# Wide cross-attention: output products in three products of high and low parts, raw expert weights loaded one stage later

## What is computed

```python
xn = _layernorm(x, ln_gamma, ln_beta)
q = (xn @ w_q).reshape(B, SQ, 16, 64)
k, v = jnp.split(context @ w_kv, 2, axis=-1)      # 16 heads of 64
attn = softmax(einsum('bqhd,bkhd->bhqk', q * 64 ** -0.5, k))
out = einsum('bhqk,bkhd->bqhd', attn, v).reshape(B, SQ, 1024)
out = (out @ w_out + b_out) * jnp.tanh(gate[0])   # 1024 -> 128
x = x + out
# sparse experts: 8 experts, top 2, hidden 352
gate = silu(einsum('td,ehd->teh', xt, W1)); up = einsum('td,ehd->teh', xt, W2)
```

## Time and profile before

| | |
|---|---|
| median of three runs | 3040.72 us |
| the profiled execution | 3037.89 us, span 3036.1 us |
| mean granted clock of PE | 0.962 |
| busy over the whole span | PE 90%, DVE 69%, POOL 64%, ACT 63% |
| stage x0, both parts | from about 462 to 1262 us |
| first batch and last batch in LAST | 529.2 and 1237.5 us |
| stage f0 begins | 1267.3 us |

### The profile page before, as it was taken

How to read it: one execution, slowest core, us unless ns; L and a number is a source line. 1 busy time by engine, 2 the same in 40 slices (tenths; PEclk the granted TensorE clock), 3 DMA queues, 4 the chain that set the end, 5 groups by cost and what they waited for, 6 DMA issues and landing times. The chain is left out here.

```text
span 3036.1 us, 83028 instructions
## 1 busy us (share of the span) xinstructions
PE 2738.4 (90%) x27974; PEld 2320.1 (76%) x27975; DVE 2097.9 (69%) x4496; ACT 1920.1 (63%) x4300; POOL 1943.3 (64%) x3244
## 2 busy tenths in 40 slices
PE   6999997999999999499997999995899999999996
PEld 5788776888888888388885888883677777777775
DVE  3677655667676766445555999997777878778543
ACT  3566553666666666355553777774878777787762
POOL 4456543456666666416667999984676777867652
PEclk9999997999999999699998999995899999999998
DMA  5566561000000000222222000000000000000000
GB/s 153 169 181 190 170 181 36 2 8 12 14 13 13 12 14 13 71 67 82 81 82 62 1 0 0 0 1 1 1 2 9 5 8 5 5 9 5 8 5 11
DMA packets 204792, 129.08 MB, mean 43 GB/s; under 512 B 13840, under 2 KB 197112, under 8 KB 203896
## 3 DMA queue, kind: packets, MB, share of 16 engines
q1 hardware_dynamic: 196344, 108.80, 12.0%
q0 software_dynamic: 8192, 16.79, 1.9%
HBM read 35.05 MB, written 90.51 MB: 41 GB/s over the span
## 5 line engine op out<-in xcount | busy, mean ns | idle before, releaser
L1552 PE MATMUL a_ps_s<-a_qk,w_ident 128*128 128x256 f32 x1024 | 238.5, 387 | 20.2 <-POOL a_qk L1659 19.1
L1007 POOL TENSOR_TENSOR x_p<-x_p,x_rz 128x1232 f32<-128x1232 f32 x64 | 143.9, 2248 | 165.6 <-DVE x_rz L1116 165.6
L584 DVE TENSOR_REDUCE a_nmax<-a_ps_s 128x4 f32<-128x512 f32 x256 | 164.9, 686 | 113.8 <-PE a_ps_s L373 113.7
L1659 POOL TENSOR_TENSOR a_qk<-a_qkv 128x2048 f32<-128x2048 f32 x64 | 235.6, 3681 | 2.6 <-POOL a_eight L218 1.0
L457 ACT ACTIVATE a_e<-a_ps_s 128x512 f32<-128x512 f32 x256 | 138.9, 595 | 152.8 <-PE a_ps_s L378 152.8
L1552 PEld LDWEIGHTS a_ps_s<-a_qk,w_ident 128*128 128x128 f32 x1024 | 192.0, 193 | 50.4 <-POOL a_qk L1659 22.7
L2374 POOL TENSOR_TENSOR x_sq<-x_e 128x1232 f32<-128x1232 f32 x64 | 143.2, 2238 | 126.2 <-DVE x_t_sq L2533 126.1
L1633 ACT ACTIVATE a_r<-a_o,w_a_rows 128x128 f32<-128x128 f32 x512 | 220.5, 521 | 1.6 <-DVE a_o L1718 1.6
L1387 POOL DMA_INDIRECT f_yg<-f_rows_out,f_index x120 | 114.9, 958 | 152.1 <-DVE f_yo L1467 134.4
L889 ACT ACTIVATE x_uu_hi<-x_ps_u 128x308 fp32r<-128x308 f32 x256 | 101.7, 423 | 106.0 <-PE x_ps_u L752 105.8
L1123 DVE TENSOR_REDUCE x_top<-x_ps_s 128x16 f32<-128x1232 f32 x64 | 91.2, 1424 | 111.2 <-PE x_ps_s L752 111.2
(11 more groups left out here) (626 smaller groups left out, 9742.0 us busy)
## 6 DMA issues: line engine op xcount, KB each, us to landing
f_rows_in<-a_zeros SPq DMA_DIRECT2D x31, 1088.0 KB, 5.4
f_rows_out<-a_zeros SPq DMA_DIRECT2D x31, 1088.0 KB, 8.8
f_xin<-f_rows_in SPq DMA_DIRECT2D x135, 64.0 KB
f_rows_out<-f_yo SPq DMA_DIRECT2D x135, 64.0 KB, 1.6
out<-x SPq DMA_DIRECT2D x16, 256.0 KB, 2.4
f_raw<-in_late_f SPq DMA_DIRECT2D x2, 1408.0 KB, 5.9
w_ctx<-in_ctx SPq DMA_DIRECT2D x1, 2464.0 KB
f_rows_in<-f_xr,f_where POOLq DMA_INDIRECT x128, 2.3
```

The costliest lines, as they stand in the source:

```text
L584: nc.vector.tensor_reduce(nmax[:, u % 2, g, :], ps_s[g][:, :].rearrange("p (t k) -> p t k", t=GROUP), AX.X, ALU.max, negate=True).then_inc ...
L1007: nc.gpsimd.tensor_tensor(wide, wide, rz[:, :].unsqueeze(2).broadcast_to([P, HEADS, K]), ALU.mult).then_inc(p_ready, 1)
L1552: ins = nc.tensor.matmul(ps_s[u % 2][:, 0:HEADS * HEADS], c.ident[:, :], qk[:, u % 2, k, :, :], start=k == 0, stop=k == HD - 1)
L1659: nc.gpsimd.tensor_tensor(qk[:, u % 2, :, :, :], qkv[:, u % UNROLL, 0, :, :].unsqueeze(3).broadcast_to(full), qkv[:, u % UNROLL, 1, :, :]. ...
```

## The change

The operands of LAST are split. The output weights `x0_o` become a pair of F32R tiles. In `wide_weights` DVE scales the raw output weights in place, ACT copies them to the high part, DVE subtracts to the low part. In each slot ACT still copies `ps_o` to the high part of `oT`, now with the semaphore `o_hi_ready`, and DVE makes the low part from `ps_o` minus the high part in two halves, with `oT_ready`. The half 0 stands behind the subtraction of the maximum in DVE's list, the half 1 behind the low parts of `projected` 2 and 3. LAST on PE makes three F32R matmuls for each of the eight float32 ones.

The load of the raw first expert weights leaves stage x0, and stage f0 issues it between the plan and the second weights, into a buffer of its own. ACT waits for it before its first split. The raw copies of keys and context on POOL have one buffer where they had two, with two waits on POOL's own earlier steps.

```diff
@@ wide_weights, scalar
+            act.wait_ge(gated_out, 1)
+            nc.scalar.activation(c.x0_o[0][:, :, :], c.w["x0_out"][:, :, :], ACT.Copy).then_inc(out_hi, 1)
@@ wide_weights, vector
-            nc.vector.tensor_scalar(c.x0_o[:, :, :], c.w["x0_out"][:, :, :], tg[:, 0:1], None, ALU.mult).then_inc(done, 1)
+            nc.vector.tensor_scalar(c.w["x0_out"][:, :, :], c.w["x0_out"][:, :, :], tg[:, 0:1], None, ALU.mult).then_inc(gated_out, 1)
...
+            dve.wait_ge(out_hi, 1)
+            nc.vector.tensor_tensor(c.x0_o[1][:, :, :], c.w["x0_out"][:, :, :], c.x0_o[0][:, :, :].bitcast(F32), ALU.subtract).then_inc(done, 1)
@@ cross_attention_wide
-        oT = sb("oT", [P, 2, PAIRS, P])
+        oT = [sb(f"oT_{n}", [P, 2, PAIRS, P], F32R) for n in ("hi", "lo")]
...
-        @block.sync
-        def _(sp):
-            sp.dma_start(c.f0_raw[:, :], c.inp["late_f0_1"]).then_inc(raw_in, 16)
-            sp.wait_ge(raw_in, 16)
@@ PE, LAST
                     for n in range(PAIRS):
-                        ins = nc.tensor.matmul(ps_y, oT[:, u % 2, n, :], c.x0_o[:, n, :], start=n == 0, stop=n == PAIRS - 1)
+                        hi, lo = (t[:, u % 2, n, :] for t in oT)
+                        nc.tensor.matmul(ps_y, hi, c.x0_o[0][:, n, :], start=n == 0, stop=False)
+                        nc.tensor.matmul(ps_y, hi, c.x0_o[1][:, n, :], start=False, stop=False)
+                        ins = nc.tensor.matmul(ps_y, lo, c.x0_o[0][:, n, :], start=False, stop=n == PAIRS - 1)
                     ins.then_inc(y_ps, 1)
@@ ACT, outputs
-                nc.scalar.activation(oT[:, u % 2, 4 * half:4 * half + 4, :], ps_o[:, :].rearrange("p (n q) -> p n q", n=4),
-                                     ACT.Copy).then_inc(oT_ready, 1)
+                nc.scalar.activation(oT[0][:, u % 2, 4 * half:4 * half + 4, :], ps_o[:, :].rearrange("p (n q) -> p n q", n=4),
+                                     ACT.Copy).then_inc(o_hi_ready, 1)
@@ POOL
+                        wait(pool, keys_lo_ready, s)
...
+                    wait(pool, cx_lo_ready, s)
@@ DVE
+            def outputs(at, half):
+                s, u = at
+                dve.wait_ge(o_hi_ready, 2 * s + half + 1)
+                hi, lo = (t[:, u % 2, 4 * half:4 * half + 4, :] for t in oT)
+                nc.vector.tensor_tensor(lo, ps_o[:, :].rearrange("p (n q) -> p n q", n=4), hi.bitcast(F32), ALU.subtract).then_inc(oT_ready, 1)
...
                                             ALU.subtract).then_inc(d_ready, 1)
+                if at := sl.step(VALUE):
+                    outputs(at, 0)
                 if at := sl.step(ROUTE):
...
                     projected(at, (2, 3))
+                if at := sl.step(VALUE):
+                    outputs(at, 1)
                 if at := sl.step(NORM):
@@ sparse_experts
-        raw = (c.f0_raw, sb("raw2", [D, E * H]))
+        raw = [sb(f"raw{n + 1}", [D, E * H]) for n in range(2)]
...
             sp.dma_start(plan[:, :], c.inp["late_f0_plan"]).then_inc(plan_in, 16)
-            sp.dma_start(raw[1][:, :], c.inp["late_f0_2"]).then_inc(raw_in, 16)
+            for n in range(2):
+                sp.dma_start(raw[n][:, :], c.inp[f"late_f0_{n + 1}"]).then_inc(raw_in[n], 16)
...
             for n in range(2):
-                if n == 1:
-                    act.wait_ge(raw_in, 16)
+                act.wait_ge(raw_in[n], 16)
                 nc.scalar.activation(w_hi[n][:, :], raw[n][:, :], ACT.Copy).then_inc(split_hi, 1)
```

More of the change, by code:

```diff
@@ L637, in wide_weights @@
         tg = sb("tg", [P, 1])
-        ready, gated, a_hi, a_lo, v_hi, done = (sem(n) for n in ("ready", "gated", "a_hi", "a_lo", "v_hi", "done"))
+        ready, gated, a_hi, a_lo, v_hi, done, gated_out, out_hi = (sem(n) for n in ("ready", "gated", "a_hi", "a_lo", "v_hi", "done", "gated_out", "out_hi"))
         block = ctx.enter_context(nc.Block())
@@ L697, in cross_attention_wide @@
         half, minus, one = (c.powers[:, k, 0:4] for k in (0, 1, 3))
-        raw, cx_raw = sb("raw", [P, 2, BATCHES, K]), sb("cx_raw", [P, 2, K])
+        raw, cx_raw = sb("raw", [P, BATCHES, K]), sb("cx_raw", [P, K])
         cx = [sb(f"cx_{n}", [P, 2, K], F32R) for n in ("hi", "lo")]
@@ L724, in cross_attention_wide @@
                  "u_ready", "cx_raw_ready", "cx_hi_ready", "cx_lo_ready", "v_ps", "v_ready", "s_ps", "max_done", "d_ready",
-                 "exp_done", "z_done", "rz_done", "p_ready", "pT_ps", "pT_ready", "o_ps", "oT_ready", "y_ps", "x_done", "biased")
+                 "exp_done", "z_done", "rz_done", "p_ready", "pT_ps", "pT_ready", "o_ps", "o_hi_ready", "oT_ready", "y_ps", "x_done", "biased")
         (xn_ready, xT_ps, xT_ready, x_hi_ready, x_lo_ready, raw_ready, keys_hi_ready, keys_lo_ready, u_ps, u_hi_ready,
          u_ready, cx_raw_ready, cx_hi_ready, cx_lo_ready, v_ps, v_ready, s_ps, max_done, d_ready,
-         exp_done, z_done, rz_done, p_ready, pT_ps, pT_ready, o_ps, oT_ready, y_ps, x_done, biased) = (sem(n) for n in names)
+         exp_done, z_done, rz_done, p_ready, pT_ps, pT_ready, o_ps, o_hi_ready, oT_ready, y_ps, x_done, biased) = (sem(n) for n in names)
         names = ("scaled", "xr_ready", "rT_ps", "rT_ready", "r_ps", "r_ready", "own", "mask_ready", "pos_ps", "pos_ready", "pos_read", "placed",
@@ L993, in slot @@
                         wait(pool, u_ps, 4 * (s - 4))
-                        nc.gpsimd.tensor_copy(raw[:, u // 4, :, :], c.ctx[:, bass.ds(s, BATCHES), :]).then_inc(raw_ready, 4)
+                        wait(pool, keys_lo_ready, s)
+                        nc.gpsimd.tensor_copy(raw[:, :, :], c.ctx[:, bass.ds(s, BATCHES), :]).then_inc(raw_ready, 4)
                         hi, lo = (t[:, u // 4, :, :] for t in keys)
                         pool.wait_ge(raw_ready, s + 4)
-                        nc.gpsimd.tensor_tensor(hi, raw[:, u // 4, :, :], one[:, 0:1].unsqueeze(2).broadcast_to([P, BATCHES, K]), ALU.mult).then_inc(keys_hi_ready, 4)
+                        nc.gpsimd.tensor_tensor(hi, raw[:, :, :], one[:, 0:1].unsqueeze(2).broadcast_to([P, BATCHES, K]), ALU.mult).then_inc(keys_hi_ready, 4)
                         pool.wait_ge(keys_hi_ready, s + 4)
-                        nc.gpsimd.tensor_tensor(lo, raw[:, u // 4, :, :], hi.bitcast(F32), ALU.subtract).then_inc(keys_lo_ready, 4)
+                        nc.gpsimd.tensor_tensor(lo, raw[:, :, :], hi.bitcast(F32), ALU.subtract).then_inc(keys_lo_ready, 4)
                 if sl.fixed and sl.t == SPLIT:
@@ L1005, in slot @@
                     pool.wait_ge(rz_done, s + 1)
+                    wait(pool, cx_lo_ready, s)
                     wide = p[:, u % 2, :, :, :].rearrange("p g j k -> p (g j) k")
                     nc.gpsimd.tensor_tensor(wide, wide, rz[:, :].unsqueeze(2).broadcast_to([P, HEADS, K]), ALU.mult).then_inc(p_ready, 1)
-                    nc.gpsimd.tensor_copy(cx_raw[:, u % 2, :], c.ctx[:, s, :]).then_inc(cx_raw_ready, 1)
+                    nc.gpsimd.tensor_copy(cx_raw[:, :], c.ctx[:, s, :]).then_inc(cx_raw_ready, 1)
                     hi, lo = (t[:, u % 2, :] for t in cx)
                     pool.wait_ge(cx_raw_ready, s + 1)
-                    nc.gpsimd.tensor_tensor(hi, cx_raw[:, u % 2, :], one[:, 0:1].broadcast_to([P, K]), ALU.mult).then_inc(cx_hi_ready, 1)
+                    nc.gpsimd.tensor_tensor(hi, cx_raw[:, :], one[:, 0:1].broadcast_to([P, K]), ALU.mult).then_inc(cx_hi_ready, 1)
                     pool.wait_ge(cx_hi_ready, s + 1)
-                    nc.gpsimd.tensor_tensor(lo, cx_raw[:, u % 2, :], hi.bitcast(F32), ALU.subtract).then_inc(cx_lo_ready, 1)
+                    nc.gpsimd.tensor_tensor(lo, cx_raw[:, :], hi.bitcast(F32), ALU.subtract).then_inc(cx_lo_ready, 1)
                 if at := sl.step(SPLIT):
@@ L1224, in sparse_experts @@
         ps_list = ps_t
-        names = ("raw_in", "w3_in", "plan_in", "split_hi", "split_lo", "late", "own",
+        raw_in = [sem(f"raw_in{n + 1}") for n in range(2)]
+        names = ("w3_in", "plan_in", "split_hi", "split_lo", "late", "own",
                  "value_ready", "list_ps", "listed", "xT_ps", "hi_ready", "lo_ready", "g_ps", "u_ps", "sg_ready", "act_ready",
                  "aT_ps", "aT_ready", "y_ps", "y_ready", "padded", "summed", "added")
-        (raw_in, w3_in, plan_in, split_hi, split_lo, late, own,
+        (w3_in, plan_in, split_hi, split_lo, late, own,
          value_ready, list_ps, listed, xT_ps, hi_ready, lo_ready, g_ps, u_ps, sg_ready, act_ready,
@@ L2631, in decoder @@
                 c.f0_xr, c.f0_where = sb("f0_xr", [P, 8, D], life=sorting), sb("f0_where", [P, 2, 2, 4], mybir.dt.uint32, sorting)
-                c.f0_raw = sb("f0_raw", list(inp["late_f0_1"].shape), life=sorting)
             if life is start:
@@ L2635, in decoder @@
                 c.x0_v = [sb("x0_v_" + n, [P, HEADS * 64], F32R, first) for n in ("hi", "lo")]
-                c.x0_o, c.x0_b = sb("x0_o", [P, HEADS // 2, D], life=first), sb("x0_b", [P, D], life=first)
```

(2 more changed lines are left out.)

1 line of the change is left out of this document (removed).

## The result

The changed kernel takes 3127.66 us in the median (3116.91 to 3135.63), the kernel before 3040.47 us in the runs beside it: ratio 1.0287, 95% interval 1.0258 to 1.0315. The time lies inside the range of 3048 to 3130 us, but 37 us above the forecast of 3090.8: +87 us where the working had summed +50. The direction and the main mechanism were right; something worth as much as three quarters of the forecast growth was not in the sum.

What follows compares the result with a forecast made beforehand. PE was taken to bound stage x0, with little idle time. Sixteen groups of four slots (+48.6 us) and f0 (+1.5) raise the profiled 3037.9 to 3088.0; the median lies 2.8 higher: 3090.8 us, range 3048 to 3130.

Steps and rivals of the forecast that it cites:

- The price of a product: LAST on PE: 24 F32R products at 0.113 us each take 2.71 us, 0.90 us more in each slot.
- the rivals built on streaming and on slow products: LAST's products on PE: streaming bound, 0.065 us each, 3054 us, chance 0.08; slow, 0.226 us each, 3252 us, chance 0.16.
- A group of four slots: Stage x0: four slots grow by 3.04 us, PE's added time less old waits plus new waits for DVE.
- both old waits: PE's waits in x0: 0.42 us for POOL's keys (third slot), 0.88 for DVE's low parts (fourth); both should go.
- the new wait: `outputs` half 1 on PE waits 0.37 us for DVE's low part in the third and fourth slots.
- 64 sequences are 16 such groups: +48.6 us: Stage x0: the 3.04 us growth of one group of four slots, taken 16 times.
- The fill and drain slots: Slots that fill and empty x0's pipeline have more idle time; left out, 2 us less if they hide two LASTs.
- `wide_weights` and POOL's waits at nothing: Added `wide_weights` steps cost nothing (1.4 us without cover); POOL's two new waits nothing, at most 0.05 us each.
- f0, +1.5 us (0 to 4): Stage f0: the moved load of 1.44 MB pushes everything behind it in the queue by 3.4 us; cost +1.5 us.
- a DVE chain longer than followed: x0: one more microsecond of DVE wait in third and fourth slots, 3123 us; chance 0.12 together with unoverlapped loads.

Runs made afterwards that it cites:

- the kernel with 16 products: Changed kernel with VectorE's loop written out, without the product of high part and low weights, low parts kept: ratio 1.0097 to the kernel before.
- each kernel with the moved body: Changed kernel with 67 more pure VectorE waits, ahead of the first slot (ratio 1.0238) or at the fourth slot's end (1.0221, both to the kernel before).
- the written-out ones with 24 products: Changed kernel with the cross-attention loop written out, for VectorE alone (3090.86 us) or for all four engines (3093.38 us).
- the one without low parts: Changed kernel with VectorE's loop written out, without VectorE's low parts of the attention outputs, 24 products kept: ratio 1.0121 to the kernel before.
- the second kernel with the moved body: Changed kernel with 67 pure VectorE waits at the end of the fourth slot, where VectorE is idle: ratio 1.0221 to the kernel before.
- the kernel with the longer body: Kernel before with 32 more instructions, pure waits already met, in VectorE's cross-attention loop body: 3041.23 us, ratio 0.9997.
- the one with the moved load: Kernel before with only the raw weights' load moved into the sparse experts' stage: ratio 1.0003.

## Why the prediction was right or wrong

- **The price of a product** (taken 0.113 us, bounds 0.065 to 0.226): right, 0.11 us. The row that decided was the right one to choose, an old pass with the same weights and columns. The trace speaks against both spacings that the Trainium skill gives in "TensorE: Matmul & The Clock Gate", section "Back-to-back issue gap", 56 and 81 ns, for these weights; the rivals built on streaming and on slow products fall with it.
- **A group of four slots** (+3.04 us): right, 3.12. Its parts: plain slots 11.95 as said; both old waits gone; the sum begins 779.15 - 776.81 = 2.34 us into the third slot (said 2.3); the low part is ready at 8.07 (said 8.1); the new wait is 0.46 and 0.42 us (said 0.37); `rank` starts 10.2 us into its slot (said 10.4). That the growth of PE is absorbed in part is shown for the third slot by the kernel with 16 products; its fourth slot ran on a chip where that slot is slower, and shows nothing.
- **"64 sequences are 16 such groups: +48.6 us":** here is the error. Multiplying one group by 16 treats all groups as alike, and every second group inside the loop contains the jump back. Its rows were in the trace of before (12.98 us where its like takes 11.06), and I read only a group without a jump. DVE's steps were costed by their busy time and by the waits that they meet, and its 31 more instructions at nothing. With the gap at the jump, the 56 distances from the eighth slot with scores to the last grew by 71.5 us; with VectorE's slots written out, by 47.5.
- **The fill and drain slots** (left out, as "2 us less" at most): wrong in sign. LAST runs in four slots of the fill too and lengthens each by 0.9 (10.8 to 11.7), with no wait that absorbs it; the two slots ahead of these take 26.0 us here, 24.0 before, and 22.7 in the same changed kernel on another chip. The drain takes 4 us more. Up to the eighth slot and behind the last, x0 grew by 9.6 us, so that 71.5 and 9.6 make up its 81.
- **`wide_weights` and POOL's waits at nothing:** right within what can be read; the first score product comes 32.2 us behind `wide_weights`' first product in both kernels.
- **f0, +1.5 us (0 to 4):** the mechanism was right and the size was in its range:

```profile
1350.87 2.55 ACT L1362 ACTIVATE f_w_hi<-f_raw 128x2816 fp32r<-128x2816 f32 x1 [13.66 <-DMA f_raw<-in_late_f]
...
1354.44 6.07 DVE L1460 TENSOR_TENSOR f_w_lo<-f_raw,f_w_hi 128x2816 fp32r<-128x2816 f32 x2
...
1361.51 0.45 PE L1347 MATMUL f_ps_x<-w_ident,f_xin 128*128 128x128 f32 x1 [7.73 <-DMA f_xin<-f_rows_in]
```

  The stage begins at 1343.7; the split starts 7.2 us behind it (said 7.2), DVE at 10.7 (said 10.7), and PE at 17.8 against 17.0, now behind the first rows of the loop rather than behind DVE. The stage is 0.6 us longer.
- **The rivals:** one, a DVE chain longer than followed, gave 3123 us and comes close to the 3127.7 measured. It was right for another reason than its own: in the ordinary groups no wait in the third and fourth slots was a microsecond longer. The cause, a fetch, was in none of them. That the time lies inside the range is owed to the ends set by these rivals, not to a term for what happened.

Why the gap costs more in the changed kernel than in the kernel before (up to 5.9 us a jump, 5.3 in the mean, in place of 2.0) is shown in part. DVE is then late for two things that PE waits for, the low parts of the score weights and those of the outputs, 1.15 + 1.21 us, and PE's clock falls behind them: 24 us at half clock are up to 12 of the 24 us by which the slots with the gap grew more than those written out. Why the clock falls behind such a wait in some slots and not in others stays open, and no run holds the clock fixed, so the split between waits and clock is worked out and not measured.

## What to carry to other kernels

Before multiplying the growth of one period by its count, list the length of every period of the loop, and cost the one with the jump back by itself. Count the instructions that a change adds to each engine's loop body, waits too: an engine with much idle time may still be pushed over a block of its instruction memory, which shows as idle time with "issue" as its cause and as more packets of the instruction queue. And a wait on the busiest matmul engine can cost more than its length, so look at the granted clock right behind it.

## What the runs showed of the hardware

**A jump back can cost VectorE 3.5 us.** Bodies at these places of its program (counted from its first instruction), by the runs:

```
first  last   instructions   gap at each jump   q14 packets
864    1155   292            none               86
864    1187   324            none (at most 0.2) 87
931    1222   292            3.6 to 3.8 us      107
901    1223   323            3.5 to 3.8 us      107, 108
968    1290   323            none (at most 0.4) 88, 88
```

Some twenty packets more for four jumps are five a jump, of 8 KB each (0.88 MB / 107), two of them inside the gap and one right behind it. Blocks of 256 instructions with one beginning between 932 and 966, and so the next between 1188 and 1222, explain all five rows, if two blocks are held: the bodies with a gap reach into a third. Other sizes were not excluded. The Trainium skill, "Runtime: NRT & Kernel Launch", section "Instruction fetch mechanics", states such a window (32 KiB in blocks of 16 KiB, 256 instructions) and that a taken branch out of it forces a fetch; the runs agree, and add the price of 3.5 to 3.8 us. The branch instruction itself shows nothing of it (50 to 80 ns in both kernels): the time stands before the instruction behind it.

**An F32R product of 128 columns with 128x128 weights costs 0.11 us**, as much as one pass of a float32 product of that size, so three F32R products for two float32 passes are half as much again on PE.

**The clock fell to 1.2 GHz behind some waits of PE of about 1.2 us**, for 3.4 us at a time or twice that. It did so at each of the changed kernel's jumps, once in each kernel with the moved body and seven times in the one with 16 products. The kernel before, the written-out ones with 24 products and the one without low parts show none from 560 to 1240 us. Most such waits pass without a fall: the second kernel with the moved body has eleven of 1.08 to 1.21 us for the low parts, and the clock fell behind one. The low part isn't its only occasion: the kernel with the longer body and the one with the moved load, neither of which has that wait, show it at one jump each, for 3.4 us, and two of the seven stand right behind PE's own pause of 2.0 us at a jump.
